# First and last FFN and last attention over four to six PSUM banks, with a new order of all engines

## The reference

```python
x = x + 0.5 * _L0_ffn_ref(_layernorm(x, axis=-1), L0_ffn_w_gate, L0_ffn_w_up, L0_ffn_w_down)
x = x + _L0_attn_ref(_layernorm(x, axis=-1), ...)          # a selective scan (Mamba)
x = x + 0.5 * _L0_ffn_ref(_layernorm(x, axis=-1), L0_ffn_w_gate, L0_ffn_w_up, L0_ffn_w_down)
x = x + 0.5 * _L1_ffn_ref(_layernorm(x, axis=-1), ...)     # base linear plus 8 gated LoRA experts
x = x + _L1_attn_ref(_layernorm(x, axis=-1), ...)          # 16 heads, ALiBi, causal softmax
x = x + 0.5 * _L1_ffn_ref(_layernorm(x, axis=-1), ...)
```

## Time and profile before

| | us |
|---|---|
| median of 3 runs | 4466.68 (4452.18 to 4469.84) |
| the profiled execution | 4467.98 |
| its span, first to last instruction | 4466.2 |
| PE, DVE, ACT, POOL busy | 3996.4, 3880.8, 2371.0, 1726.5 |
| mean granted clock of PE | 0.962 of full |

### The profile page before, as it was taken

The page is one execution under the profiler, slowest core; times in us unless marked ns, Lnnn a source line. Parts: engine busy times, 40 slices in busy tenths (PEclk is TensorE's granted clock), DMA queues, the critical chain, the costliest instruction groups (busy, mean ns, idle before and its releaser), DMA issues.

```text
span 4466.2 us, 55876 instructions
## 1 busy us (share of the span) xinstructions
PE 3996.4 (89%) x19107; PEld 2067.6 (46%) x19107; DVE 3880.8 (87%) x5708; ACT 2371.0 (53%) x4341; POOL 1726.5 (39%) x1293
## 2 busy tenths in 40 slices
PE   5878889999999999998989999899989999989998
PEld 3333444444545444454544445454544445444453
DVE  7698989898999989999898999899898989988622
ACT  2444455655555565655556565646556555555333
POOL 1154534343434434444343434444443434434200
PEclk9988999998999999999999999999999989999998
DMA  2698788867788877886887787797787678778301
GB/s 62 154 213 199 170 202 171 199 148 182 182 167 200 177 194 164 195 190 158 196 179 187 168 201 171 168 224 159 191 186 183 166 180 192 157 195 177 84 27 29
DMA packets 241440, 753.51 MB, mean 169 GB/s; under 512 B 37650, under 2 KB 132659, under 8 KB 171524
## 3 DMA queue, kind: packets, MB, share of 16 engines
q1 hardware_dynamic: 241156, 749.95, 71.9%
HBM read 647.30 MB, written 101.71 MB: 168 GB/s over the span
## 4 chain that ended last, share of the span: by engine, by line
PE 41%; DVE 33%; DMA 9%; ACT 8%; issue 6%; SPq 2%; POOL 1%; DVEq 0%; ACTq 0%; POOLq 0%
DVE state L1723 9%; PE m L1207 6%; DVE mt L1800 5%; PE m L1234 4%; DVE u L1718 4%; DMA decay<-dt_scratch 3%; PE pd L1433 3%; DMA state<-dtx_scratch 3%; PE y L1296 3%; PE y L1308 2%; DVE front L1657 2%; PE pg L1411 2%; PE pu L1411 1%; ACT decay L1008 1%; PE m L1264 1%
## 5 line engine op out<-in xcount | busy, mean ns | idle before, releaser
L787 POOL TENSOR_TENSOR state<-state,bc 128x1024 f32<-128x1024 f32 x512 | 1266.1, 2473 | 1305.5 <-DVE u L1718 1304.3
L1723 DVE TENSOR_TENSOR_SCAN state<-decay,u 128x1024 f32<-128x1024 f32 x512 | 1166.2, 2278 | 6.2 <-ACT decay L1008 0.9
L1207 PE MATMUL m<-w_gu,hats_m 128*128 128x480 f32 (+1 forms) x1536 | 716.4, 587 | 74.7 <-DVE front L1632 46.7
L1008 ACT ACTIVATE decay<-decay,a_neg 128x511 f32<-128x511 f32 x1024 | 672.7, 713 | 176.1 <-DMA decay<-dt_scratch 175.3
L1718 DVE TENSOR_TENSOR u<-state,bc 128x1024 f32<-128x1024 f32 x512 | 642.5, 1255 | 34.7 <-DMA state<-dtx_scratch 25.9
L1207 PEld LDWEIGHTS m<-w_gu,hats_m 128*128 128x128 f32 x1536 | 270.2, 194 | 356.1 <-issue 161.7
L1154 PE MATMUL y<-minus,zero 128*128 128x512 bf16 x1549 | 414.3, 391 | 2.1 <-ACT vec L862 2.1
L1234 PE MATMUL m<-w_dn,front 128*128 128x256 f32 x1536 | 385.4, 392 | 18.3 <-ACT front L941 17.7
L768 POOL TENSOR_TENSOR front<-front,hsc_m 128x704 f32<-128x704 f32 x128 | 195.9, 1530 | 511.5 <-DVE front L1537 500.5
L1296 PE MATMUL y<-state,sel 128*32 128x512 f32 x2048 | 285.8, 633 | 56.4 <-POOL state L787 56.1
L1234 PEld LDWEIGHTS m<-w_dn,front 128*128 128x128 f32 x1536 | 282.0, 193 | 102.7 <-ACT front L941 51.7
(11 more groups left out here) (266 smaller groups left out, 7115.3 us busy)
## 6 DMA issues: line engine op xcount, KB each, us to landing
decay<-dt_scratch SPq DMA_DIRECT2D x256, 1024.0 KB, 7.4
state<-dtx_scratch SPq DMA_DIRECT2D x256, 1024.0 KB, 11.6
qk_scratch<-shared SPq DMA_DIRECT2D x64, 384.0 KB, 3.7
shared<-qk_scratch SPq DMA_DIRECT2D x384, 64.0 KB
kh<-qk_scratch SPq DMA_DIRECT2D x384, 64.0 KB
xs_scratch<-front SPq DMA_DIRECT2D x16, 1024.0 KB, 9.9
dt_scratch<-front SPq DMA_DIRECT2D x256, 64.0 KB, 2.6
dtx_scratch<-hats_m SPq DMA_DIRECT2D x256, 64.0 KB, 5.9
```

The lines of the kernel that those rows point to most:

```text
L787: eng.tensor_tensor(st, st, bc[:, 1:2, :].to_broadcast([P, WIDE, L]), ALU.mult).then_inc(scan_pool.sem, scan_pool.step(f"c{r}{h}"))
L1008: ins = eng.activation(d, d, ACT.Exp, scale=a_neg[:, g:g + 1])
L1207: mm = eng.matmul(f.bank(f"gu{t}{p}")[:, 0:2 * width], norm.hat_t[:, k, t * P:(t + 1) * P], w_gu[:, k, 2 * lo:2 * (lo + width)], start=(k ...
L1723: eng.tensor_tensor_scan(st, decay[:, n % ND, h * WIDE * L:(h + 1) * WIDE * L], u[:, :], 0.0, ALU.mult, ALU.add).then_inc(scan_dve.sem, sc ...
```

## The change

FFN 0 takes six banks (m0, m1, both of u, pg, pu), FFN 31 four (m0, m1, both of u), all others two as before. Attention 15 takes six (pg, pu, m0, m1, both of u), all others two. `free` waits for the use that many places back. DVE's division gets one wait more, for the division before it. All five tables of ORDER are new; on PE there are 1718 keepers instead of 1654, and all other instructions are as many as before. The diff, with two rows of the tables and the places that repeat `f.bank(r, ...)` or `att_bank(r, ...)` left out:

```diff
--- before.py
+++ after.py
@@ -74,167 +74,168 @@
 ORDER = {
     "SP":
...
     "POOL":
...
-        "22233323111111122220222211110112222012222111011112222112222111111222211133332222222200222222220022222222222222222222222222222222",
+        "33331111222211111011222202222111101222212222101111122221112212211111222233330222202222022222222022222222222222222222222222222222",
...
 }
...
 
-                self.banks = banks
+                self.banks, self.first, self.last = banks
                 self.xn = part(0, I)
                 self.size = part(1024, I)
                 self.th = part(1024 + I, I)
@@ -353,8 +354,12 @@
 
                 self.uses = ["x0", "x1"] + gu(0) + [n for t in range(T) for n in (gu(t + 1) if t < T - 1 else []) + [f"ht{t}", f"dn{t}"]]
 
-            def bank(self, use):
-                return self.banks[self.uses.index(use) % len(self.banks)]
+            def banks_of(self, r):
+                return self.first if r == 0 else self.last if r == len(FFNS) - 1 else self.banks
+
+            def bank(self, r, use):
+                banks = self.banks_of(r)
+                return banks[self.uses.index(use) % len(banks)]
 
         MB = [pb(f"m{n}") for n in range(2)]
         Y = pb("y")
@@ -363,7 +368,8 @@
         RB = [PG, PU, PD, Y]
         shared = sb("shared", [P, SHARED])
         front = sb("front", [P, FRONT])
-        f = Ffn("m", front, MB)
+        U = [u[:, 0:L], u[:, L:2 * L]]
+        f = Ffn("m", front, (MB, MB + U + [PG, PU], MB + U))
 
         def part(at, n):
             return shared[:, at:at + n]
...
         att_events = [n for k in range(NG) for n in scores_of(k) + [w for w in after_group(k) if w[0] != "p"]]
-        att_bank = {n: (PG, PU)[k % 2] for k, n in enumerate(att_events)}
-
-        def heads(event, width, n):
-            return att_bank[event][:, 0:n * width].rearrange("p (g l) -> p g l", g=n)
+        att_banks = lambda r: [PG, PU] + (MB + [u[:, 0:L], u[:, L:2 * L]] if r == B - 1 else [])
+
+        def att_bank(r, event):
+            banks = att_banks(r)
+            return banks[att_events.index(event) % len(banks)]
+
+        def heads(r, event, width, n):
+            return att_bank(r, event)[:, 0:n * width].rearrange("p (g l) -> p g l", g=n)
...
+                    eng.activation(m_rows[:, :], att_bank(r, f"m{j}")[0:3 * G, :], ACT.Copy).then_inc(att_act.sem, att_act.step(f"m{j}"))
...
+                        eng.activation(pt[:, slot:slot + n, 0:width], heads(r, f"e{j}{t}{g}", width, n), ACT.Exp
...
             def free(r, use):
-                before = f.uses.index(use) - len(f.banks)
+                before = f.uses.index(use) - len(f.banks_of(r))
                 if before >= 0:
...
-                            mm = eng.matmul(f.bank(f"gu{t}{p}")[:, 0:2 * width], norm.hat_t[:, k, t * P:(t + 1) * P],
+                            mm = eng.matmul(f.bank(r, f"gu{t}{p}")[:, 0:2 * width], norm.hat_t[:, k, t * P:(t + 1) * P],
                                             w_gu[:, k, 2 * lo:2 * (lo + width)], start=(k == 0), stop=(k == KD - 1))
...
-                    down = f.bank(f"dn{t}")
+                    down = f.bank(r, f"dn{t}")
                     for part, (lo, hi) in (("a", (0, 4)), ("b", (4, IK))):
                         yield
                         if part == "a":
                             eng.wait_ge(f.pool.sem, f.pool.after(r, f"rescaled{t}"))
                             free(r, f"ht{t}")
-                            dst = f.bank(f"ht{t}")[:, 0:4 * P]
+                            dst = f.bank(r, f"ht{t}")[:, 0:4 * P]
                         else:
                             free(r, f"dn{t}")
                             dst = down[:, D:D + 2 * P]
...
-                    before = att_events.index(event) - 2
+                    before = att_events.index(event) - len(att_banks(r))
                     if before >= 0:
...
                             eng.matmul(out, qh[0:MAXROW, b, g + h, t * P:(t + 1) * P], kh[0:MAXROW, b, g + h, 0:width], start=(h == 0), stop=True, skip_group_check=True)
...
-                        bank, cols = f.bank(f"gu{t}{p}"), slice(lo, lo + width)
+                        bank, cols = f.bank(r, f"gu{t}{p}"), slice(lo, lo + width)
                         eng.wait_ge(f.act.sem, f.act.after(r, f"th{t}{p}"))
...
-                    o = att_bank[f"ot{j}"][:, :].rearrange("p (t g c) -> p t g c", t=T, g=G)
+                    o = att_bank(r, f"ot{j}")[:, :].rearrange("p (t g c) -> p t g c", t=T, g=G)
                     eng.wait_ge(att_pe.sem, att_pe.after(r, f"ot{j}"))
+                    if j or r:
+                        eng.wait_ge(att_dve.sem, att_dve.after(r, f"att{j - 1}") if j else att_dve.after(r - 1, f"att{J - 1}"))
                     eng.reciprocal(rec[:, :, :], o[:, :, :, HD]).then_inc(att_dve.sem, att_dve.step(f"rec{j}"))
                     yield
```

More of the change, by code:

```diff
@@ L901, in ffn @@
                 yield
-                yield from evac_hat(f.act, r, f.pe, normed("front" if front else "back", n)[0].hat_t, (f.bank("x0"), f.bank("x1")))
+                yield from evac_hat(f.act, r, f.pe, normed("front" if front else "back", n)[0].hat_t, (f.bank(r, "x0"), f.bank(r, "x1")))
                 def tanh(t):
@@ L917, in tanh @@
                             eng.wait_ge(f.dve.sem, f.dve.after(r - 1, f"s{T - 1}{p}"))
-                        eng.activation(f.th[:, lo:lo + width], f.bank(f"gu{t}{p}")[:, 0:width], ACT.Tanh).then_inc(f.act.sem, f.act.step(f"th{t}{p}"))
+                        eng.activation(f.th[:, lo:lo + width], f.bank(r, f"gu{t}{p}")[:, 0:width], ACT.Tanh).then_inc(f.act.sem, f.act.step(f"th{t}{p}"))
                 yield from tanh(0)
@@ L939, in low @@
                         eng.wait_ge(f.low_pe.sem, f.low_pe.after(r, f"ht{t}{part}"))
-                        src = f.bank(f"ht{t}")[:, 0:4 * P] if part == "a" else f.bank(f"dn{t}")[:, D:D + 2 * P]
+                        src = f.bank(r, f"ht{t}")[:, 0:4 * P] if part == "a" else f.bank(r, f"dn{t}")[:, D:D + 2 * P]
                         eng.activation(f.h_t[:, lo:hi, :], src.rearrange("p (k n) -> p k n", n=P), ACT.Copy
@@ L944, in low @@
                     eng.wait_ge(f.low_pe.sem, f.low_pe.after(r, f"dn{t}"))
-                    eng.activation(x[:, t, :], f.bank(f"dn{t}")[:, 0:D], ACT.Copy).then_inc(f.low_act.sem, f.low_act.step(f"res{t}"))
+                    eng.activation(x[:, t, :], f.bank(r, f"dn{t}")[:, 0:D], ACT.Copy).then_inc(f.low_act.sem, f.low_act.step(f"res{t}"))
             def head(i):
@@ L1195, in ffn @@
                 banks_free("front" if front else "back", n)
-                yield from hat_transposes(norm, f.pe, (f.bank("x0"), f.bank("x1")))
+                yield from hat_transposes(norm, f.pe, (f.bank(r, "x0"), f.bank(r, "x1")))
                 def gate_up(t):
@@ L1406, in scores @@
                     for h in range(n):
-                        out = heads(event, width, n)[:, h, :]
+                        out = heads(r, event, width, n)[:, h, :]
                         if w == "s":
```

321 lines of the change are left out of this document (160 added, 161 removed).

## The result

Four executions of the changed kernel took 4397.07 us in the median (4387.96 to 4411.94), against 4467.6 of before; the ratio of the two kernels on record is 0.9862 with a 95% interval of 0.9829 to 0.9895 (the quotient of these two medians alone would be 0.984). Timed again it was 0.9885 (0.9862 to 0.9908). By the two ratios the kernel is 1.2 to 1.4% faster, 51 to 62 us; the forecast was 19, and 4397 lies under its range, which began at 4426. The profiled execution took 4389.99 us, with a mean granted clock of 0.980 instead of 0.962.

The account below looks back on a forecast made before the run. The prediction took DVE to pace the middle and PE mostly the end; -5.0, -2.9, 0, -4 and -7 summed to -18.9 us from the 4466.68 median, 4448 us, with a range of 4426 to 4472 (the forecast's own 4435 to 4461).

Parts of the forecast that it names:

- First FFN: Start of the kernel: six banks instead of two let stats of head 0 start at 112.7 instead of 117.77, -5.0 us.
- The first scan step: Head: u and its scan move into DVE's 16.5 us idle hole before the logarithm, -2.9 us.
- The middle: 430 to 4077 us, sixteen overlapping sequences: same instructions, some neighbours swapped, 0 us, with 11 us allowed either way.
- My own sign of being wrong: DVE's idle time between the head of sequence 1 and the last scan changing by more than 11 us.
- rival 2: The middle gains too: 7% of DVE's 280 idle us go, -20 us more, 4428 us; chance 0.15.
- Last scan to last FFN: 4163 to 4283 us: last sums together, FFN brought forward, attention 14 put back, PE deciding; -4 us.
- Last attention: From 4357 us on: six banks instead of two, more keepers and a higher PE clock give -7 us.
- rival 1: End of the kernel: the attention chain holds it, sum 0, 4467 us; chance 0.23 together with the no-bank-effect rival.
- (3): SP's queue: scan loads wait behind attention loads, each round 0.18 us more, 42 us in all, 4490 and above; chance 0.10.
- (4): Banks have no effect and order is neutral, 4464 us; chance 0.23 together with the attention-chain rival.

Follow-up runs that it names:

- banks_only: The changed kernel's code and banks with all five order tables of the kernel before; 0.9979 of the kernel before.
- att_banks: The kernel before with six banks for the last attention alone, both FFNs at two, all tables old; 0.9974 of the kernel before.
- middle_only: The changed kernel's banks, new tables for scans 1 to 13 only, tables of before elsewhere; 0.9920 of the kernel before.
- fill_chain: The kernel before with ten keepers more in each attention, five ahead of each of two waits at its end; 0.9978 of the kernel before.
- after_fill: The changed kernel with ten keepers more in each attention, at the two waits at its end; 0.9876 of the kernel before.
- after_again: The changed kernel itself, unaltered, timed a second time beside its parts on one chip; 0.9885 of the kernel before.
- tail_only: The changed kernel's banks, tables of before up to the start of scan 14, new tables from there to the end; 0.9954 of the kernel before.

## Why the prediction was wrong, step by step

**First FFN, -5.0.** Right: stats of head 0 start at 112.38 instead of 117.77, -5.4. What of it reaches the end cannot be told: banks_only, with stats at some 3 us earlier, is no faster than att_banks.

**The first scan step, -2.9.** The mechanism ran as described: the first u at 167.83 (I said near 167) instead of 179.30, behind a load that landed 11.6 us after its issue, and a hole of 14.65 us left. The gain was not kept. A later u waits 6.21 us for its state load at 195.28, and scan 0 takes 200.5 us instead of 194.3. The first scan began 11.9 us earlier and scan 1 only 5.8, no more than the first FFN had given. What was mis-sized is the term: 0 was left of it.

**The middle, 0 within 11.** This is the step that failed: the term was put at nothing, and the order there, with its keepers, is worth 26 us by middle_only, 21 to 25 of them in scans 1 to 6. My own sign of being wrong, DVE's idle time, shows it: in scans 1 to 6 it is 80 to 97 us in the eight traces of the new order and 102 to 123 in the six of the old. I argued that the same instructions, with DVE busy for 92%, leave nothing to swapped neighbours, and gave rival 2 a chance of 0.15. The earlier trace rows said already that PE is as full as DVE there, 3336 of 3647 us or 91%, so that its pace counts too; I took DVE alone as the limit. And I did not cost the clock: PE in the earlier trace rows is at 0.97 there, and 0.01 of 3647 us is 36 us if all of it reached the end, which is an upper bound. I weighed the clock at the last attention only.

How much of it reaches the end is not settled. Over 111 executions of the kernel before, a mean clock higher by 0.01 goes with 34 us less, and by that line the changed kernel's 0.975 to 0.977 against 0.965 would make 32 to 40 of its 51 to 62 us. But one more execution, left out of the line, recorded 0.927 and took 4472.76 us, some 115 less than the line gives; with it the line falls to 16 us. And where keepers raised the clock, the time did not follow the line: fill_chain, 0.009 higher, should have gained 30 us and gained 9; after_fill, 0.006 higher than after_again, should have gained 20 and gained 4, within noise. Clock and time move together, and less waiting also raises the clock. What is shown is that the two waits of fill_chain pull the clock down, and that the middle without any keepers has a lower clock and is some 100 us slower.

**Last scan to last FFN, -4.** Wrong as put, right in sum. From the last scan sum to attention 15 the changed kernel needs 3.9 us more. The gain stands ahead of it: scan 14 is 18 us shorter, since attention and lora work that DVE and PE did in it (231.43 busy instead of 236.16, 231.54 instead of 248.60) is done later. PE's rows at the end of the last scan:

```profile
4093.60 2.11 PE L1306 MATMUL y<-state,sel 128*32 128x512 f32 x16
4096.52 1.99 PE L1318 MATMUL y<-w_out,skip 128*128 128x256 f32 x8 [0.81 <-DVE skip L1711]
...
4104.06 1.89 PE L1318 MATMUL y<-w_out,skip 128*128 128x256 f32 x8
...
4106.22 1.88 PE L1381 MATMUL pg<-hats_r,w_q 128*128 128x512 f32 x4
```

The last two sums together, output products directly behind, then the projections: as read from the order. tail_only puts the order from scan 14 to the end at -11 us, that of the last attention included. I had counted from 4154.76 on and missed what the shift frees before.

**Last attention, -7.** Right mechanism, mis-sized: -13.5. The banks alone make it 62.7 us instead of 73.0 (att_banks 62.3), 10.3 us where I gave them 2.7 with the pace of DVE's maxima as limit. The new order with its 41 keepers brings about 2 us more. The new keepers alone cost 3.2 us, where rival 1 had 6. The granted clock of this attention rose from 0.84 to 0.89 (0.92 in att_banks) with the banks and no keeper added. That bears on the rule weighed in the prediction, the Trainium skill's "TensorE: Matmul & The Clock Gate", section "A second HAM failure mode: psum-queue depth-cycling", by which small idle spells between groups that cycle through banks pull the clock down: the traces agree in direction, though deeper rotation alone did not bring it wholly to its higher level. The other section I set against it, by which more PSUM buffers gain nothing once PE is kept warm, never had its condition here: with 41 keepers on two banks the clock was still at 0.87, and they lost 3.2 us; six banks with 13 keepers won 10.3.

**Rivals.** The attention chain did not hold the end (1); the middle gained (2), by 26 us where 20 were worked out, and it was DVE's idle time that went, as the rival had it; SP's queue cost little beyond the first rounds (3), for DVE's product waited 20.7 us for its loads in the middle, in 21 waits, instead of 16.4 in 18; the banks had an effect (4). The range ended where rival 2 did, without adding the tail's and the last attention's larger terms to it.

## What to carry to other kernels

Where two engines are both nine tenths busy, a new order of the same instructions can shorten a stretch, and its worth should not be put at nothing without a look at both engines: here it was 25 us of 1511. Where PE is one of the two and its granted clock is under 1, ask also what the order does to the clock, but don't count the whole of it: here a us less at half clock went with 0.32 us less of time. Look behind every short chain that PE waits on, since waits of 1.1 and 1.5 us were followed by 7 to 27 us at half clock. Fill matmuls belong to the order they were laid for, and are laid again when it moves.

## What the runs showed unlooked for, and what stays open

Keepers moved to the same steps of another order cost 90 to 100 us, as much as leaving out all 1001 of the middle. Two halves of scans 1 to 6 bring nothing each that the times can tell, and 21 to 25 us together; their own scans got shorter in their traces, so whether the halves really don't add stays open. Which of the moved steps in scans 1 to 6 make the gain, the part with the clock and the part without it, stays open, and so does what the new order would be worth with other keepers. The measured parts (banks 9, scans 1 to 6 21 to 25, tail 11) make 41 to 45 us of the 51 to 62; the rest lies within their uncertainties.
